# Router choice and sends of two batches moved from the tail into a scan, and a stage's first loads issued in the stage before it

## The chip, the cores and the metric

The kernel runs on one core of one Trainium2 chip. The metric is device time in microseconds (us) of one execution. Besides the time of plain runs there is one profiled execution, whose trace gives each instruction its start and duration. Engines are called as in the profile: PE (TensorE), DVE (VectorE), ACT (ScalarE), POOL (GpSimd) and SP (SyncE, which here only issues DMAs).

## What is computed

The reference works on x of 4 batches x 512 tokens x 512 features and a context of 4 x 512 x 256. Four layers are added to x in turn:

```python
x = x + _L0_xattn_ref(_layernorm(x), fside_BxS2xS2_0, ctx_1024)   # two int8-quantised linears, silu gate
x = x + _L0_ffn_ref(_layernorm(x), lut, gate_idx, up_idx, down_idx)  # weights = lut[idx], width 1376
x = x + _L1_xattn_ref(ctx_1024, _layernorm(x), ...)               # selective scan, 16 states x 512 channels
x = x + _L1_ffn_ref(_layernorm(x), gate_w, w_gate, w_up, w_down)  # 32 experts, 8 of them per token

def step(state, inp):                       # the scan, over the 512 positions
    d, b, c, u = inp
    dA = jnp.exp(d[..., None] * A)
    state = state * dA + (d * u)[..., None] * b[:, None, :]
    y = jnp.einsum('bdn,bn->bd', state, c)

probs = jax.nn.softmax(x @ gate_w, axis=-1)     # the expert layer, P = tokens * 8, E = 32
w, sel = jax.lax.top_k(probs, K)
pos = jnp.arange(P) - start[se]                 # a row's place among the rows of its expert
y = jnp.einsum('eci,eih->ech', silu(g) * u, w_down)
out = jnp.zeros((T + 1, H)).at[t_slot].add(w_slot[:, None] * y)
```

## The kernel before

The program is two blocks with a barrier of all engines between them. `front_block` computes the first layer, makes the looked-up weights of the second layer in 176 slots of a small PE product each, stores them to DRAM (`w_halves`), and stores what the scan reads: dt, du, u, the rows of B and C (`bc_rows`), and x after the first layer (`x_store`). SP issues nearly all DMAs of the block, in the order of its code. At its end SP waits for the landing of all stores of dt, u, B and C and x, and for the zero fills of the send buffer (`filled`, lines 369 to 373), so the barrier opens after the last store has landed.

`mix_and_experts_block` has three stages.

**The scan** runs 4 batches of 16 slots, slot g = 16 b + l (`UNITS` = 16). In a slot POOL makes the scan's input for the slot ahead (`inputs_product`, line 1441, B times du), ACT makes four decays exp(dt A) into a single PSUM bank (line 1895), DVE does four scans (line 2217) and two products with C (line 2225, after the second and the fourth scan), PE sums the states (line 1637). A decay waits for the scan before it, since both use the one bank. In the room beside that PE computes the second layer, from slot 3 of each batch on: `up` products (line 1611), `down` products (line 1625), with ACT and DVE forming the half between them. Layer norms, z gates and residuals are put in by slot number, as "asides" of ACT and lines between DVE's scans. SP issues the weight loads (`mix_wup`, `mix_wdn`) one or two halves ahead and the loads of B and C of the next batch in slots 13 to 15.

**The tail**, after the last slot: the last residual and z gate, and the router for all 16 tiles of 128 tokens. Per batch PE transposes the normalised rows and multiplies with `gw` (`choice_transposes`, `logits`), DVE subtracts the maximum (`shift`, line 2304), ACT takes the exponent, DVE finds the top 8 (`choose`), PE counts the ranks, DVE turns them into row numbers (`place`, line 2341 writes `where`). POOL then sends the rows: 128 indirect DMAs (`send`, line 1474), 16 tiles for each of k = 0 to 7, where k is the rank of the choice in the order of expert numbers. A token's k-th expert is never below k, so expert e can be loaded once the sends of k up to e are done; SP waits for that, for e under 8, and loads the tiles (line 1357).

**The experts**: 32 times, 576 rows each in five tiles: PE transposes (line 1763), gate and up (line 1793), down (line 1816), ACT writes the split activations (line 2015 once per half), the result goes back by DMA. The sends of k = 2 to 7 run beside the experts 0 to 5, each k after expert k-2's tiles are transposed. From expert 6 on POOL adds results to the output (line 1492).

## Time and profile before

| | us |
|---|---|
| median of 3 runs | 1883.29 (1882.07 to 1884.48) |
| the profiled execution | 1881.68 |
| its span in the trace | 1879.5 |
| first block, to the barrier | 0 to about 510 |
| scan | 533 to about 1181 |
| tail, to the first tile load | 1181 to 1239 |
| experts 0 to 6 | 1239 to about 1411 |
| the remaining experts, end | 1411 to 1879.5 |

Busy shares over the span: PE 83%, DVE 70%, ACT 48%, POOL 42%. The mean DMA rate is 237 GB/s.

In a timeline row stand the start (us from the span's start), the duration, the engine, the line, the operation with output<-input, and in brackets the idle time before it with what released it. A row of `SPq` is a DMA being issued, not its transfer. In a table of stretches stand the stretch, its length, the busy time and number of instructions of PE, PEld (weight loads), DVE, ACT and POOL, and then the granted PE clock (1.00 is 2.4 GHz), the DMA share of 16 engines and GB/s. A DMA row ends with KB each and the median us from issue to landing.

### The profile page before, as it was taken

The numbers are of one execution on the slowest core, as the hardware profiler recorded it, in microseconds if no ns is written. First come the engines' busy times: TensorE is split into PE (matmuls) and PEld (weight loads), VectorE is DVE, ScalarE is ACT, GpSimd is POOL, SyncE is SP. The second block draws the span as 40 slices with busy tenths as digits, with TensorE's granted clock in tenths as the row PEclk, the third lists the DMA queues.
The fourth block names the chain that finished last, engine by engine and source line by source line (L and its number), as shares of the span: only waits on it lengthen the run. The fifth ranks groups of instructions, "written<-read, shape, count | busy, mean of one in ns | idle before, by whom it ended". The sixth has DMA issues, their size and how long they took to land. (4 is left out here: it accounts for less than half of the span.)

```text
span 1879.5 us, 26432 instructions
## 1 busy us (share of the span) xinstructions
PE 1554.0 (83%) x9418; PEld 1319.2 (70%) x9426; DVE 1308.7 (70%) x1901; ACT 911.0 (48%) x1577; POOL 791.8 (42%) x481
## 2 busy tenths in 40 slices
PE   5857778677528987996898799975899999999896
PEld 3444355454428976895897689855789999999785
DVE  6677586786659989999998999642445555555452
ACT  3444545445234444344444534432466666666463
POOL 1010000010045456445655643177735766762555
PEclk9878888888758997997999799987999999999998
DMA  7988799984682492375359236379998999999876
GB/s 213 343 281 275 274 321 368 333 270 157 210 314 95 175 357 74 119 283 222 106 188 370 82 118 218 145 266 338 382 365 232 250 269 253 256 260 223 226 170 85
DMA packets 187942, 445.48 MB, mean 237 GB/s; under 512 B 41616, under 2 KB 43664, under 8 KB 177568
## 3 DMA queue, kind: packets, MB, share of 16 engines
q1 hardware_dynamic: 115040, 283.37, 44.7%
q0 software_dynamic: 31760, 74.48, 16.8%
q10 hardware_dynamic: 41008, 85.89, 12.6%
q8 instruction: 78, 1.28, 0.3%
q14 instruction: 56, 0.46, 0.1%
HBM read 246.77 MB, written 205.28 MB: 241 GB/s over the span
## 5 line engine op out<-in xcount | busy, mean ns | idle before, releaser
L1441 POOL TENSOR_TENSOR mix_st<-mix_Bb,mix_du 128x2048 f32<-128x2048 f32 x64 | 293.3, 4583 | 268.2 <-DVE mix_st L2225 255.7
L2217 DVE TENSOR_TENSOR_SCAN mix_st<-mix_YY,mix_st 128x512 f32<-128x512 f32 x256 | 312.0, 1219 | 46.0 <-POOL mix_st L1441 24.0
L1895 ACT ACTIVATE mix_YY<-mix_dt,mix_A 128x512 f32<-128x512 f32 x256 | 176.9, 691 | 276.5 <-DVE mix_st L2217 272.3
L1492 POOL DMA_INDIRECT out_x<-moe_ys,moe_meta x130 | 210.5, 1619 | 190.1 <-ACT moe_ys L2032 84.6
L1611 PE MATMUL mix_G<-mix_xThi,mix_wup 128*128 128x256 f32 x1408 | 273.0, 291 | 14.5 <-issue 13.6
L1611 PEld LDWEIGHTS mix_G<-mix_xThi,mix_wup 128*128 128x128 f32 x1408 | 231.8, 199 | 17.6 <-issue 16.2
L1793 PE MATMUL mix_Dp<-moe_xhi,moe_whi 128*128 128x288 f32 x768 | 234.5, 305 | 2.0 <-ACT moe_xhi L1995 1.5
L1793 PE MATMUL mix_Dp<-moe_xhi,moe_wlo 128*128 128x288 f32 x768 | 228.9, 298 | 0.0
L1793 PE MATMUL mix_Dp<-moe_xlo,moe_whi 128*128 128x288 f32 x768 | 228.7, 298 | 0.0
L2357 DVE TENSOR_TENSOR moe_xlo<-mix_G,moe_xhi 128x512 fp32r<-128x512 f32 (+1 forms) x160 | 102.2, 638 | 170.5 <-ACT moe_xhi L1995 167.9
L1637 PE MATMUL mix_YY<-mix_ident,mix_st 128*128 128x128 f32 x1024 | 145.1, 296 | 86.2 <-DVE mix_st L2225 86.2
L435 PE MATMUL front_L<-front_oh,front_pick 128*128 128x512 f32 x528 | 177.9, 475 | 45.0 <-ACT front_wst L582 28.6
L1611 PE MATMUL mix_G<-mix_xTlo,mix_wup 128*128 128x256 f32 x704 | 203.9, 290 | 0.0
L1637 PEld LDWEIGHTS mix_YY<-mix_ident,mix_st 128*128 128x128 f32 x1024 | 126.0, 153 | 99.3 <-issue 52.6
L742 DVE TENSOR_SCALAR front_oh<-front_idx,front_kcol 128x1536 fp32r<-128x1536 int32 x176 | 176.6, 1048 | 13.8 <-PE front_L L435 10.4
L435 PEld LDWEIGHTS front_L<-front_oh,front_pick 128*128 128x128 f32 x528 | 109.9, 220 | 94.7 <-DVE front_oh L742 39.6
L2225 DVE TENSOR_TENSOR mix_st<-mix_st,mix_Cb 128x1024 f32<-128x1024 f32 x128 | 161.5, 1262 | 1.1
L1793 PEld LDWEIGHTS mix_Dp<-moe_xhi,moe_whi 128*128 128x128 f32 x768 | 146.7, 191 | 8.1 <-issue 2.2
L1474 POOL DMA_INDIRECT x_by_expert<-moe_XB,moe_where x128 | 129.1, 1009 | 46.3 <-issue 38.9
L1793 PEld LDWEIGHTS mix_Dp<-moe_xlo,moe_whi 128*128 128x128 f32 x768 | 146.7, 191 | 2.3
L1793 PEld LDWEIGHTS mix_Dp<-moe_xhi,moe_wlo 128*128 128x128 f32 x768 | 146.4, 191 | 0.0
L2347 DVE TENSOR_TENSOR moe_wlo<-moe_raw,moe_whi 128x768 fp32r<-128x768 f32 (+1 forms) x96 | 100.2, 1045 | 64.0 <-ACT moe_whi L1984 64.0
(237 smaller groups left out, 3064.9 us busy)
## 6 DMA issues: line engine op xcount, KB each, us to landing
x_by_expert<-front_zeros ACTq DMA_DIRECT2D x16, 4480.0 KB, 24.1
mix_wup<-w_halves SPq DMA_DIRECT2D x44, 1024.0 KB, 5.5
moe_raw<-in_ew SPq DMA_DIRECT2D x32, 1280.0 KB, 8.5
moe_xt<-x_by_expert SPq DMA_DIRECT2D x128, 256.0 KB, 8.6
mix_wdn<-w_halves SPq DMA_DIRECT2D x44, 512.0 KB, 6.4
front_idx<-in_idx SPq DMA_DIRECT2D x44, 384.0 KB, 9.0
w_halves<-front_wst SPq DMA_DIRECT2D x44, 384.0 KB, 7.9
mix_Bb<-bc_rows SPq DMA_DIRECT2D x16, 1024.0 KB, 9.4
```

The source lines that it names most:

```text
L435: last = nc.tensor.matmul(L[:, n, :], pick[:, j, :, :].rearrange("p a n -> p (a n)"), oh[:, t % OH, n * S:(n + 1) * S], start=(j == 0), st ...
L742: nc.vector.tensor_scalar(oh[:, t % OH, :], idx[:, h % 2, :], kcol[:, j:j + 1], None, ALU.is_equal).then_inc(onehot_made, 1)
L1441: nc.gpsimd.tensor_tensor(st[:, g % STBUF, :, :], Bb[:, q, :, :], du[:, k % 2, :].unsqueeze(1).to_broadcast([P, NG, S]), ALU.mult).then_in ...
L1474: pool.indirect_dma_start(out=s["XG"], out_offset=bass.IndirectOffsetOnAxis(ap=where[:, i, k:k + 1], axis=0), in_=XB[:, i, :], in_offset=N ...
L1492: pool.indirect_dma_start(out=out_rows, out_offset=bass.IndirectOffsetOnAxis(ap=meta[0:rows, e % MBUF, j, 0:1].bitcast(U32), axis=0), in_= ...
L1611: last = nc.tensor.matmul(G[:, i % 2, v, :], wup[:, j % UPBUF, part, v * D + c * P:v * D + (c + 1) * P], x[:, c, cols], start=(n == 0), st ...
L1637: last = nc.tensor.matmul(Y[:, t, :], st[:, g % STBUF, n, t * P:(t + 1) * P], ident[:, :], is_transpose=True, start=(q == 0 and n == 0 and ...
L1793: last = nc.tensor.matmul(Dp[:, m % 4, 0:HALF_U], w[:, e % 2, at:at + P], x[:, e % 2, c, cols], start=(n == 0), stop=(n == len(steps) - 1))
L1895: nc.scalar.activation(dA, dt[:, k % 2, :], ACT.Exp, scale=A[:, c, m:m + 1]).then_inc(da_ready, 1)
L2217: nc.vector.tensor_tensor_scan(r, dA, r, 0.0, ALU.mult, ALU.add).then_inc(scanned, 1)
L2225: nc.vector.tensor_tensor(r, r, Cb[:, l % GROUPS, own, :], ALU.mult).then_inc(prod_ready, 1)
L2357: nc.vector.tensor_tensor(xlo[:, e % 2, :, at], T[:, n % 2, :].rearrange("p (c t) -> p c t", c=DC)[:, :, 0:rows], xhi[:, e % 2, :, at].bit ...
```

## The change

**Seam between the blocks.** `load_ahead` is new in the first block: at slot turn 170, behind the 19th pair of weight stores, SP waits for all stores of dt, u, B and C and issues the first loads of the scan (dt, du, four of B, x of batch 0; 5.5 MB) into SBUF which a new layout leaves free. The block's end waits for `filled` alone; the landing of x of the last batches (`x1_out`) is waited for in `load_x(b)` of the second block and by DVE before the first residual. In the second block SP's first issues are A, dskip and four loads of C; POOL's first instruction is the product of slot 0, ahead of the small memsets, which ACT and DVE wait for no longer.

**Early choice.** The router of batches 0 and 1 (`EARLY` = 2) is computed in batches 2 and 3 of the scan. PE: transposes of tile 0 and 1 in slot 15 of batches 1 and 2, of tile 2 and 3 and all logits in slot 0 of batches 2 and 3, ranks in slot 2. ACT: the copies of the transposes (`rows_to_columns`), the first of them ahead of the decay for the next slot; exponent in slot 1. DVE: shift, top 8 and mask in slot 1, place in slot 3, weights in slot 4. SP stores row numbers and weights behind the rows (`store_meta`, slot 5) and loads three of four tiles back (`load_waiting`).

**Sends in the scan.** 48 of the 128 sends (three tiles of each of the two batches, all k) are issued by POOL in slots 8 to 15 and the next slot 0 of batch 2, and in slots 9 to 15 and right behind the scan of batch 3. Each k after that has 10 sends instead of 16: two tiles of the early batches, four of batch 2, four of batch 3. The tail chooses for batches 2 and 3 alone.

```diff
+AHEAD_AT = 170
+SENDS_AT = ({8: 3, 9: 2, 10: 3, 11: 3, 12: 3, 13: 3, 14: 3, 15: 3, 16: 1}, {9: 2, 10: 3, 11: 3, 12: 3, 13: 3, 14: 3, 15: 3, 16: 4})
...
+            def load_ahead():
+                sp.wait_ge(bc_out, 16 * NB)
+                sp.wait_ge(u_out, 16 * NB)
+                sp.wait_ge(dt_out, 32 * NB)
+                sp.dma_start(dt[:, 0, :], s["DT"][0][:, 0, :]).then_inc(ahead_in, 16)
+                sp.dma_start(du[:, 0, :], s["DU"][0][:, 0, :]).then_inc(ahead_in, 16)
...
+                sp.dma_start(xt_mix[:, 0, :, :], s["X1"][0].rearrange("(t p) n -> p t n", p=P)).then_inc(ahead_in, 16)
...
-            sp.wait_ge(bc_out, 16 * NB)
-            sp.wait_ge(u_out, 16 * NB)
-            sp.wait_ge(dt_out, 32 * NB)
-            sp.wait_ge(x1_out, 16 * NB)
             sp.wait_ge(filled, 16 * (FILLS + 2))
...
+            def send_waiting(w, first, end):
+                if first == 0:
+                    pool.wait_ge(filled, 16 * (FILLS + 2))
+                    pool.wait_ge(waiting_in, 16 * w + 16)
+                    pool.wait_ge(where_ready, w + 1)
+                for j in range(first, end):
+                    k, n = divmod(j, STAGED)
+                    send(w * STAGED + n, k, waiting[w][:, n, :])
...
-            for k in range(TOP):
+            sends(EARLY, 0)
+            sends(EARLY + 1, 0)
+            for k in range(1, TOP):
                 if k > 1:
                     pool.wait_ge(e_xT_ready, NT * (k - 2) + 2)
-                for b in range(NB):
-                    sends(b, k)
+                sends_on_chip(k)
+                sends(EARLY, k)
+                sends(EARLY + 1, k)
...
+                    if l == UNITS - 1 and 0 < b <= EARLY and t == 3:
+                        rows_to_columns(b - 1, 0)
+                    if l == 0 and b >= EARLY and t != 1:
+                        rows_to_columns(b - 2, max(1, t))
+                    if l == 1 and b >= EARLY and t == 1:
+                        exponent(b - 2)
...
+                if l == 1 and b >= EARLY:
+                    choose_top(b - 2)
+                if l == 3 and b >= EARLY:
+                    place_key(b - 2)
+                if l == 4 and b >= EARLY:
+                    row_weights(b - 2)
```

On SP around the barrier, from the last store of the first block on, before (`x_store` is x after the first layer; lines 155, 64, 63 and 1212 are the wait and the barrier):

```order
L329 DMA x_store<-front_xt 128x4x512 [waits front_x1_ready]
L155 UNCONDITIONAL_BRANCH [waits front_x1_out,front_dt_out,rows_filled,front_u_out,front_bc_out]
L64 UNCONDITIONAL_BRANCH [waits barrier_Pool_Activation_PE_DVE_SP_release]
L67 ISA
L63 UNCONDITIONAL_BRANCH
L1212 UNCONDITIONAL_BRANCH [waits barrier_Pool_Activation_PE_DVE_SP_release]
L1274 DMA mix_A<-in_alog 128x64
L1275 DMA mix_dskip<-in_dskip 128x4
L1219 DMA mix_dt<-dt_store 128x512
L1222 DMA mix_du<-du_store 128x512
L1233 DMA mix_Bb<-bc_rows 128x2048
```

And now:

```order
L366 DMA mix_dt<-dt_store 128x512 [waits front_dt_out,front_u_out,front_bc_out]
L367 DMA mix_du<-du_store 128x512
L369 DMA mix_Bb<-bc_rows 128x2048 x4
L371 DMA mix_xt<-x_store 128x4x512
L317 DMA w_halves<-front_wst 64x1536 [waits front_evicted]
...
L343 DMA x_store<-front_xt_111 128x4x512 [waits front_x1_ready]
L162 UNCONDITIONAL_BRANCH [waits rows_filled]
L64 UNCONDITIONAL_BRANCH [waits barrier_Pool_Activation_PE_DVE_SP_release]
...
L1373 DMA mix_A<-in_alog 128x64
L1374 DMA mix_dskip<-in_dskip 128x4
```

The loads of dt, du, B and x stand ahead of the last weight stores and of the barrier, and the wait for `x1_out` is gone.

On PE at the end of slot 15 of batch 1 and in slot 0 of batch 2, before (`mix_G` by `wup` is an up product, `mix_Dp` by `wdn` a down product, `mix_YY` by `mix_st` the sum of states):

```order
L1611 MATMUL mix_G<-mix_xThi,mix_wup 128x256
L1637 MATMUL mix_YY<-mix_ident,mix_st 128x128 x16
L1644 MATMUL mix_YY<-mix_ident,mix_u 128x128 x4
L1625 MATMUL mix_Dp<-mix_wdn,mix_hhi 128x512 x2
L1625 MATMUL mix_Dp<-mix_wdn,mix_hlo 128x512
```

And now (line 1808 is an early transpose, line 1822 the logits):

```order
L1747 MATMUL mix_G<-mix_xThi,mix_wup 128x256
L1808 MATMUL mix_G<-mix_ident,mix_x_3853 128x128 x4
L1773 MATMUL mix_YY<-mix_ident,mix_st 128x128 x8
L1808 MATMUL mix_G<-mix_ident,mix_x_3853 128x128 x4
L1773 MATMUL mix_YY<-mix_ident,mix_st 128x128 x8
L1780 MATMUL mix_YY<-mix_ident,mix_u 128x128 x4
L1808 MATMUL mix_G<-mix_ident,mix_x_3853 128x128 x4
L1822 MATMUL mix_G<-mix_gw,mix_y 128x32 x8
L1761 MATMUL mix_Dp<-mix_wdn,mix_hhi 128x512 x2
```

The first transposes stand behind the last up product of slot 15, and the logits ahead of the down products of slot 0.

On POOL in slots 8 and 9 of batch 2, before:

```order
L1441 TENSOR_TENSOR mix_st<-mix_Bb,mix_du 128x2048 [waits late_unit_done,late_prod_ready,late_b_in1,late_dt_du_in0]
L1441 TENSOR_TENSOR mix_st<-mix_Bb,mix_du 128x2048 [waits late_unit_done,late_prod_ready,late_b_in2,late_dt_du_in0]
L1447 TENSOR_TENSOR mix_rstd<-mix_mv,mix_eps_col 128x4 [waits late_var_ready2]
L1448 TENSOR_TENSOR mix_rstd<-mix_rstd,mix_power 128x4 [waits late_pool_link]
L1449 TENSOR_TENSOR mix_nmr<-mix_mv,mix_rstd 128x4 [waits late_pool_link]
L1450 TENSOR_TENSOR mix_nmr<-mix_zero,mix_nmr 128x4 [waits late_pool_link]
L1441 TENSOR_TENSOR mix_st<-mix_Bb,mix_du 128x2048 [waits late_unit_done,late_prod_ready,late_b_in3,late_dt_du_in0]
```

And now:

```order
L1535 TENSOR_TENSOR mix_st<-mix_Bb,mix_du 128x2048 [waits late_unit_done,late_prod_ready,late_b_in1,late_dt_du_in0]
L1581 DMA x_by_expert<-mix_waiting_3859,mix_where 33024x560 [waits late_where_ready,late_waiting_in,rows_filled]
L1581 DMA x_by_expert<-mix_waiting_3859,mix_where 33024x560 x2
L1535 TENSOR_TENSOR mix_st<-mix_Bb,mix_du 128x2048 [waits late_unit_done,late_prod_ready,late_b_in2,late_dt_du_in0]
L1549 TENSOR_TENSOR mix_rstd<-mix_mv,mix_eps_col 128x4 [waits late_var_ready2]
...
L1581 DMA x_by_expert<-mix_waiting_3859,mix_where 33024x560 x2
L1535 TENSOR_TENSOR mix_st<-mix_Bb,mix_du 128x2048 [waits late_unit_done,late_prod_ready,late_b_in3,late_dt_du_in0]
```

The sends stand between two products of POOL, two or three to a slot.

## Rows read from the trace of the kernel before

**Rows 1.** Busy time, clock, DMA share and rate of three stretches

```profile
510.00:1181.00 671.00, 558.01 (x3866) 519.95 (x3867) 604.19 (x779) 296.64 (x534) 346.11 (x127) 0.89 0.54 196
...
1393.00:1848.00 455.00, 449.63 (x2967) 405.52 (x2966) 244.73 (x405) 281.11 (x532) 258.23 (x150) 0.99 0.95 237
...
1306.00:1328.00 22.00, 17.70 (x104) 15.56 (x105) 8.01 (x14) 9.38 (x18) 16.81 (x18) 0.92 1.03 380
```

**Rows 2.** Timeline of DVE: the first scan

```profile
533.21 1.22 DVE L2217 TENSOR_TENSOR_SCAN mix_st<-mix_YY,mix_st 128x512 f32<-128x512 f32 x1 [23.99 <-POOL mix_st L1441]
```

**Rows 3.** Timeline of SP, ACT and POOL around the barrier

```profile
496.88 12.83 SPq L303 DMA_DIRECT2D w_halves<-front_wst  x4
509.75 1.21 SPq L329 DMA_DIRECT2D x_store<-front_xt  x1
519.57 0.33 SPq L1274 DMA_DIRECT2D mix_A<-in_alog  x1
...
526.07 0.69 ACT L1895 ACTIVATE mix_YY<-mix_dt,mix_A 128x512 f32<-128x512 f32 x1 [3.81 <-DMA mix_du<-du_store]
...
528.62 4.49 POOL L1441 TENSOR_TENSOR mix_st<-mix_Bb,mix_du 128x2048 f32<-128x2048 f32 x1 [8.30 <-DMA mix_Bb<-bc_rows]
```

**Rows 4.** DMA issues from 505 to 521 us: KB each, median us to landing

```profile
x_store<-front_xt SPq DMA_DIRECT2D x1, 1024.0 KB, 7.4
...
mix_A<-in_alog SPq DMA_DIRECT2D x1, 32.0 KB, 1.8
```

**Rows 5.** Timeline of ACT and PE where batch 1 ends

```profile
849.14 0.69 ACT L1895 ACTIVATE mix_YY<-mix_dt,mix_A 128x512 f32<-128x512 f32 x1 [1.28 <-DVE mix_st L2217]
...
851.53 1.91 PE L1637 MATMUL mix_YY<-mix_ident,mix_st 128*128 128x128 f32 x16
...
859.44 1.06 PE L1637 MATMUL mix_YY<-mix_ident,mix_st 128*128 128x128 f32 x8 [2.79 <-DVE mix_st L2225]
```

**Rows 6.** Two stretches of the tail: DVE's top 8 with weights, and place

```profile
1200.49:1202.54 2.05, 2.05 (x21) 2.05 (x21) 1.91 (x17) 0.60 (x1) 1.08 (x3) 1.00 0.00 0
1206.86:1208.11 1.25, 1.25 (x14) 1.25 (x14) 1.15 (x8) 0.47 (x1) 0.92 (x3) 1.00 1.03 383
```

**Rows 7.** DVE products: all in the scan, one beside POOL, experts with and without sends

```profile
L2225 DVE TENSOR_TENSOR mix_st<-mix_st,mix_Cb 128x1024 f32<-128x1024 f32 x128 | 161.5, 1262 | 1.1
...
897.87 2.07 DVE L2225 TENSOR_TENSOR mix_st<-mix_st,mix_Cb 128x1024 f32<-128x1024 f32 x1
...
L2347 DVE TENSOR_TENSOR moe_wlo<-moe_raw,moe_whi 128x768 fp32r<-128x768 f32 x10 | 9.6, 964 | 7.2 <-ACT moe_whi L1984 7.2
...
L2347 DVE TENSOR_TENSOR moe_wlo<-moe_raw,moe_whi 128x768 fp32r<-128x768 f32 x45 | 43.0, 956 | 40.6 <-ACT moe_whi L1984 40.6
```

**Rows 8.** Timeline of POOL: a product of the scan

```profile
830.48 4.62 POOL L1441 TENSOR_TENSOR mix_st<-mix_Bb,mix_du 128x2048 f32<-128x2048 f32 x1 [5.43 <-DVE mix_st L2225]
```

**Rows 9.** Landing of the up weights: whole span, then 1005 to 1020 us

```profile
mix_wup<-w_halves SPq DMA_DIRECT2D x44, 1024.0 KB, 5.5
...
mix_wup<-w_halves SPq DMA_DIRECT2D x2, 1024.0 KB, 8.8
```

**Rows 10.** The sends: their group on the page, and the fifth of them

```profile
L1474 POOL DMA_INDIRECT x_by_expert<-moe_XB,moe_where x128 | 129.1, 1009 | 46.3 <-issue 38.9
...
1221.26 0.97 POOL L1474 DMA_INDIRECT x_by_expert<-moe_XB,moe_where  x1 [6.83 <-DVE moe_where L2341]
```

**Rows 11.** Timeline of SP: the tile loads of expert 0

```profile
1238.67 2.39 SPq L1357 DMA_DIRECT2D moe_xt<-x_by_expert  x5
```

**Rows 12.** Timeline of ACT: first split activation of experts 0, 7 and 8

```profile
1255.78 0.45 ACT L2015 ACTIVATE moe_chl<-moe_hc 64x288 fp32r<-64x288 f32 x1 [0.26 <-DVE moe_hc L2368]
...
1421.33 0.43 ACT L2015 ACTIVATE moe_chl<-moe_hc 64x288 fp32r<-64x288 f32 x1
...
1438.92 0.43 ACT L2015 ACTIVATE moe_chl<-moe_hc 64x288 fp32r<-64x288 f32 x1
```

**Rows 13.** Queue of the sends from 1306 to 1328 us: packets, MB, share

```profile
q0 software_dynamic: 1286, 4.61, 52.4%
```

More of the change, by code:

```diff
@@ L959, in downs_of_slot, with mix_and_experts_block @@
     return early + halves_of_slot(g - 2)
-def mix_and_experts_block(nc, d, s, out, filled, w_out):
+def mix_and_experts_block(nc, d, s, out, filled, w_out, x1_out, ahead_in, ahead):
     ALL = NB * UNITS
@@ L1926, in normalise @@
                     act.wait_ge(zT_ready, TT * (b - 1))
+                    if b == NB - 1 and t == 0:
+                        for k in range(TOP):
+                            act.wait_ge(sent[k], 16 * STAGED)
                 nc.scalar.activation(xn[:, t, :], x[:, t, :], ACT.Identity, bias=nmr[:, w, t:t + 1],
@@ L1969, in exponent @@
                 act.wait_ge(shifted, b + 1)
-                own = pr[:, b * TT:(b + 1) * TT, :]
-                nc.scalar.activation(own, own, ACT.Exp).then_inc(exp_ready, 1)
+                nc.scalar.activation(pr(b), pr(b), ACT.Exp).then_inc(exp_ready, 1)
             def weights_high(e, c):
@@ L2310, in choose, with choose_top, choose_mask @@
+                nc.vector.tensor_tensor(pr(b), lg, over_experts(mx(b)), ALU.subtract).then_inc(shifted, 1)
+            def choose_top(b):
                 dve.wait_ge(exp_ready, b + 1)
-                for i in tiles:
-                    last = nc.vector.max(top[:, i, :], pr[:, i, :])
+                for t in range(TT):
+                    last = nc.vector.max(top(b)[:, t, :], pr(b)[:, t, :])
                 link(last)
-                for i in tiles:
-                    last = nc.vector.match_replace(rest[:, i, :], top[:, i, :], pr[:, i, :], -1.0)
+            def choose_mask(b):
+                for t in range(TT):
+                    last = nc.vector.match_replace(rest(b)[:, t, :], top(b)[:, t, :], pr(b)[:, t, :], -1.0)
@@ L2316, in choose @@
                 link(last)
[L2317 removed]
+                nc.vector.tensor_scalar(masks(b), rest(b), 0.0, None, ALU.is_lt).then_inc(mask_ready, 1)
             def row_weights(b):
[L2320 to L2322 removed]
@@ L2323, in row_weights @@
-                nc.vector.tensor_tensor(XB[:, own, D + 1:D + 1 + E_N], pr[:, own, :], over_experts(total[:, own]),
-                                        ALU.mult).then_inc(meta_ready, 1)
-            def place(b):
-                own = slice(b * TT, (b + 1) * TT)
-                tiles = range(b * TT, (b + 1) * TT)
+                link(nc.vector.tensor_reduce(total(b), top(b), AX_X, ALU.add))
+                link(nc.vector.reciprocal(total(b), total(b)))
+                to = meta_of(b)[:, :, 1:META] if b < EARLY else XB[:, b * TT:(b + 1) * TT, D + 1:D + META]
@@ L2335, in place, with place_rows, choose @@
                 dve.wait_ge(mask_ready, b + 1)
-                link(nc.vector.scalar_tensor_tensor(out=key[:, own, :], in0=key[:, own, :], scalar=-1.0,
-                                                    in1=mask[:, own, :], op0=ALU.mult, op1=ALU.mult))
-                for i in tiles:
-                    last = nc.vector.max(near[:, i, :], key[:, i, :])
-                link(last)
-                nc.vector.tensor_scalar(where[:, own, :], near[:, own, :], -1.0, AWAY, ALU.mult, ALU.add).then_inc(where_ready, 1)
+                link(nc.vector.scalar_tensor_tensor(out=key(b), in0=key(b), scalar=-1.0, in1=masks(b),
+                                                    op0=ALU.mult, op1=ALU.mult))
+            def place_rows(b):
+                for t in range(TT):
+                    last = nc.vector.max(near(b)[:, t, :], key(b)[:, t, :])
+                link(last)
+                nc.vector.tensor_scalar(where[:, b * TT:(b + 1) * TT, :], near(b), -1.0, AWAY, ALU.mult,
+                                        ALU.add).then_inc(where_ready, 1)
+            def choose(b):
+                choose_top(b)
+                choose_mask(b)
+            def place(b):
+                place_key(b)
+                place_rows(b)
             def weights_low(e, c):
```

514 lines of the change are left out of this document (322 added, 192 removed).

## The prediction

> **What bounds the kernel now.** I first read the table of stretches, because each stage has a limit of its own. In the scan DVE is busy 604 of 671 us and DMA has half its time free; in the late experts PE is busy 450 of 455 us, so nothing but PE's work counts there; in a stretch of the early experts PE has only 17.7 of 22 us and DMA is full at 380 GB/s [rows 1]. Then the timelines at the two seams. Between the blocks DVE stands idle for 24.0 us before its first scan at 533.21 [rows 2]. From the tail to the early experts I follow one mark, ACT's first split activation of an expert: expert 0 has it at 1255.78, expert 7 at 1421.33 and expert 8 at 1438.92 [rows 12]. An expert that waits for nothing takes 17.6 us; the seven before took 165.6 instead of 7 x 17.6 = 123.1, so 42.4 us are lost there, beside the tail itself. So three places matter: seam 1, the tail with experts 0 to 6, and the scan, which now gets more work.
>
> **Seam 1.** Before, the last store of x is issued at 509.75 and the first DMA of the second block at 519.57 [rows 3]; the store takes 7.4 us from its issue to landing [rows 4], so it is in at 517.15 and from there to the first issue are 2.4 us of barrier. The change takes that landing out of the barrier. SP gets there when the issue of the store ends, at 509.75 + 1.21 = 510.96 [rows 3]; with the same 2.4 the second block opens at 513.3. B and du are then in SBUF: their loads are 5.5 MB, at 380 GB/s [rows 1] 15 us, and stand ahead of the last four weight stores, which before were issued from 496.88 on [rows 3]. So POOL's product of 4.49 us [rows 3] ends at 517.8. ACT's first decay needs A: its load took 1.8 us on a free queue [rows 4], but now it stands behind the megabyte of x. I take it as landed at 517.3 to 517.9; two small instructions and the decay of 0.69 [rows 3] put the first scan at 519.4. The Trainium skill, DMA: Bandwidth & Descriptors, Queues (HWDGE ordering), says that on each DMA engine descriptors are consumed in ring order; by that rule A is behind x, with no rule A would be in at 515.1 and the product would decide, at 517.8. The sum goes by 519.4, with ends 517.8 and 519.9: 533.21 - 519.4 = 13.8. A wait of 0.7 on the load of u and the short waits for the other B loads go too: **-14.5**, from -16 to -8 if the barrier still ends with the landing. The loads' price in the first block is their issue on SP, 7 issues at under 1.2 us [rows 3] ahead of weight stores for which nobody is waiting: nothing, as PE and DVE there don't wait for SP. What is late next is the wait of DVE for `x1_out` before the first residual, hundreds of us later: nothing.
>
> **Tail.** Before, the fifth send, the first of batch 1, starts at 1221.26, 6.8 us idle and right behind the second batch's row numbers, and the tile loads of expert 0 are issued at 1238.67 [rows 10, 11]. Between are 11 more sends at 1.009 + 0.3 us = 1.28, and one landing. In the changed order batch 3 stands where batch 1 stood, with one shift and one set of weights fewer ahead, about 2.5 us: its rows are ready at about 1217.7 and its weights at 1218.4. By then batch 2's sends and the on-chip tiles' are out. Four sends (5.1 us) end at 1223.7; the load follows the last send's end by 1.9 us as before: 1225.6, **13.1** earlier.
>
> **Experts 0 to 6.** In 22 us of the early experts DMA moved 8.35 MB by 22 x 380 GB/s [rows 1], 4.61 MB of it the 16 sends of one k [rows 13]. With 10 sends, 2.88 MB, an expert has some 6.5 MB, at the same rate 17.1 us. By POOL it is 10 x 1.28 = 12.8 us instead of 20.5 [rows 10]. Both are under PE's 17.6, the first only just. I let expert 0 have its mark 13.1 earlier, at 1242.7; expert 1 takes 20.3, since PE is still at its lower clock and the loads bunch up; six at 17.6 would put expert 7 at 1368.6, 52.7 before 1421.33 [rows 12]. For a limit so near I add 5 us of waits: 1374, so tail and experts together give **-47**. Ends: -55 with no waits and a better expert 1, -30 if an expert still takes 21 us. From expert 7 on the pace is PE's in both.
>
> **What the scan pays.** (1) The first early transposes stand behind the last up product of slot 15. ACT's copy of them stands ahead of the decay for the next slot, which ran at 849.14; the up products end and PE's next group starts at 851.53 [rows 5]. So ACT waits until about 852.1, copies 0.6, and the decay starts at 852.7 to 852.9 and the scan behind it at 853.5 instead of 850.75: 2.65 us, twice: **+5.3** (bounds +2, if DVE's asides fill the hole, and +6). (2) DVE's own new work where it is the bound: the same work in the tail took 2.05 (top 8, mask, weights) and 1.25 (place) [rows 6]. With 0.1 of a wait that is 3.4 for a batch; the shift hides in DVE's wait for ACT. Twice, and 0.4 once for the last row: **+7.2** (0 to +9; slots in which PE is the bound would hide it, but slots 1 to 4 aren't such). (3) PE's transposes, logits and ranks are 4.6 us per batch, most in slot 0, where PE had idle times of 2.8 and 1.4 [rows 5] and none is waited for: 0, without this cover +2 a batch. (4) The sends: POOL has 5.4 us idle beside a 4.6 us product in a slot [rows 8] and three sends are 3.8: hidden, and POOL's product is a slot ahead. (5) Their bytes, 0.86 MB in a slot that had up to 400 GB/s in slots 13 to 15: up weights landed in 5.5 us and in 8.8 where B and C were loaded [rows 9]. I put +1 for late weights in batch 2 and +0.5 for ACT's wait for the 24 sends at the start of the last z path. Sum of the scan: 5.3 + 7.2 + 1.5 = **+14**, from +8 to +25.
>
> **The sum.** -14.5 - 47 + 14 = -47.5. The profiled execution took 1881.7, of which the span is 1879.5; 1881.7 - 47.5 = 1834.2. The median of the runs is 1.6 above the profiled one, so **1836 us**. The case's own range is 1826 to 1846.
>
> **Rival A: the early experts stay bound by DMA.** For it: DMA is at full share in them, and 17.1 is half a microsecond from PE's pace, with results and the next raw weights coming in bursts. Against it: a quarter of the bytes is gone. If an expert takes 21 us, seven take 147 instead of 165.6: 18.6, and 13.1 of the tail, 31.7 in all: 1836 + 15 = 1851.
>
> **Rival B: sends and DVE's products hold each other up.** The one product of the scan that began beside a POOL product took 2.07 us, against 1.26 in the mean [rows 7]. If the sends did the same to both products of a slot, 16 slots x 2 x 0.81 = 26 us at most; the sends fill under half of the time in which the products can fall: about 12 to 26, so 1848 to 1862, I say 1858. Against it: DVE's two-input operation on 768 columns took 964 ns in the stretch with sends and 956 without [rows 7]. The Trainium skill, SBUF — State Buffer, SBUF: two separate sides, says that a DVE operation with two SBUF inputs locks the shared port pair only against a GpSimd operation that reads SBUF, and its box on DVE and DMA lets only DVE's operations in a two-port mode starve the descriptors. By that a send costs a product nothing, by its general lock it would; the trace agrees with the first (964 and 956), so B has a small chance.
>
> **Rival C: the scan turns to its weight loads, slower than before.** The place is PE's up product, which waits for `mix_wup`. Loads are one to two slots of about 10 us ahead, and land in 5.5 to 8.8 [rows 9]. With 0.86 MB of sends more per slot they could land later than 13 us; then every us more stalls PE and with it DVE. The gain of 61.5 at the seams less the 12.5 of the early choice is 49; the 16 slots with sends must lose over 3 us each to turn it round, so landings of over 16 us: 1890. Against it: 0.86 MB at 380 GB/s is 2.3 us, and in slots 8 to 12 DMA is half idle.
>
> **Rival D: better than forecast.** The chain in slot 15 costs less, expert 1 follows at 18, no DMA limit: 1822.
>
> **That the change doesn't do what it says** can be at seam 1 alone: another engine or `filled` may end the barrier late. It costs 6 of the 14.5: 1842, within the first case.
>
> **How the numbers follow.** Forecast 0.60, A 0.20, B 0.08, C 0.04, D 0.08. The predicted time is that of the first. The range must reach to A and D, with the ends of the unknown costs around A: 1820 to 1857; left out are C, and part of B and of the ends. A measurement of this kernel can tell about 0.2%, 3.8 us. Every case but C is faster by more than that: faster 0.94; between C and the others lies a strip with 0.02; slower 0.04.
>
> **What would show it.** Right: the first scan near 519.4 and its idle time ended by ACT, not POOL; the slot behind slot 15 of batches 1 and 2 longer by 2 to 3 us with ACT waiting for PE; no product of POOL starting later than it would by DVE; the tile loads of expert 0 about 13 us nearer to the end of the scan; marks of experts 1 to 7 under 18.5 us apart and PE's waits for tiles in the early experts below 15 us. Wrong: marks over 20 us apart with DMA full (A); DVE's products over 1.5 us in slots 8 to 15 of batches 2 and 3 (B); PE idle there with the up weights as releaser (C); first scan after 524, or the scan over 20 us longer, by a chain that I have not seen between ACT's copies and PE in slot 0.

## The result

| | before | changed |
|---|---|---|
| median of 4 runs each | 1882.88 us | 1837.78 us (1835.89 to 1838.54) |
| the profiled execution | 1881.68 | 1838.54 |
| its span in the trace | 1879.5 | 1836.8 |

The ratio is 0.9758, with a 95% interval from 0.9741 to 0.9775: 45 us faster. The prediction was 1836, with a range from 1820 to 1857. The total was right to 2 us; the terms of its sum were not all, as the marks show. A mark is the same event in both traces:

| mark | before | changed | gain so far |
|---|---|---|---|
| last store of x issued (first block) | 509.75 | 511.46 | -1.7 |
| first scan | 533.21 | 520.64 | 12.6 |
| POOL's product 16 (first slot of batch 1) | 676.84 | 662.04 | 14.8 |
| last product of the scan on DVE | 1177.40 | 1175.69 | 1.7 |
| tile loads of expert 0 | 1238.67 | 1227.50 | 11.2 |
| first split activation, expert 0 | 1255.78 | 1245.93 | 9.9 |
| the same, expert 1 | 1294.27 | 1272.26 | 22.0 |
| the same, expert 7 | 1421.33 | 1379.75 | 41.6 |
| end | 1879.5 | 1836.8 | 42.7 |

So seam 1 gives 16.5 us when counted from the store of x (the first block itself ended 1.7 later), the scan takes 13.1 of it away, the tail gives 9.5, the experts 0 to 7 give 30.4, and the rest 1.1.

### The profile page after: what moved, and what is told of

Read it like the earlier page. It is cut to its first block and busy times, and to the rows that moved or that the text cites. A ratio compares the mean times of both kernels' runs of the same rounds, so it can differ in the third digit from the quotient of the medians.

```text
span 1836.8 us, 26417 instructions
## 1 busy us (share of the span) xinstructions
PE 1548.2 (84%) x9418; PEld 1317.3 (72%) x9426; DVE 1312.9 (71%) x1901; ACT 910.5 (50%) x1577; POOL 798.9 (43%) x485
## 3 DMA queue, kind: packets, MB, share of 16 engines
q8 instruction: 78, 1.28, 0.3%
## 5 line engine op out<-in xcount | busy, mean ns | idle before, releaser
L765 DVE TENSOR_SCALAR front_oh<-front_idx,front_kcol 128x1536 fp32r<-128x1536 int32 x176 | 176.6, 1048 | 13.9 <-PE front_L L458 10.3
L2398 DVE TENSOR_TENSOR mix_st<-mix_st,mix_Cb 128x1024 f32<-128x1024 f32 x128 | 165.7, 1295 | 0.9
L1747 PEld LDWEIGHTS mix_G<-mix_xTlo,mix_wup 128*128 128x128 f32 x704 | 140.1, 199 | 1.4
## 6 DMA issues: line engine op xcount, KB each, us to landing
mix_wdn<-w_halves SPq DMA_DIRECT2D x44, 512.0 KB, 7.1
```

Source lines behind the costliest of these rows:

```text
L765: nc.vector.tensor_scalar(oh[:, t % OH, :], idx[:, h % 2, :], kcol[:, j:j + 1], None, ALU.is_equal).then_inc(onehot_made, 1)
L1747: last = nc.tensor.matmul(G[:, i % 2, v, :], wup[:, j % UPBUF, part, v * D + c * P:v * D + (c + 1) * P], x[:, c, cols], start=(n == 0), st ...
L2398: nc.vector.tensor_tensor(r, r, Cb[:, l % GROUPS, own, :], ALU.mult).then_inc(prod_ready, 1)
```

## The profile of the changed kernel

**Seam 1.** Timelines of SP, ACT and POOL, to be read against [rows 2, 3]:

```profile
511.46 1.22 SPq L343 DMA_DIRECT2D x_store<-front_xt  x1
515.00 0.35 SPq L1373 DMA_DIRECT2D mix_A<-in_alog  x1
...
515.02 4.50 POOL L1535 TENSOR_TENSOR mix_st<-mix_Bb,mix_du 128x2048 f32<-128x2048 f32 x1 [18.98 <-POOLq L63]
...
519.27 0.26 ACT L2040 ACTIVATE mix_A<-mix_A 128x64 f32<-128x64 f32 x1 [2.98 <-DMA mix_dskip<-in_dskip]
...
520.64 1.22 DVE L2390 TENSOR_TENSOR_SCAN mix_st<-mix_YY,mix_st 128x512 f32<-128x512 f32 x1 [9.73 <-ACT mix_YY L2055]
```

From the store's issue to the first DMA of the second block are now 3.5 us, before 9.8. POOL starts at once and is ready at 519.5; ACT waits for the two small loads, A and dskip, until 519.27, and the first scan is released by ACT and no longer by POOL. These loads, issued at 515.00 and 515.40, show how long they took behind the megabyte of x. The page of DMA issues from 508 to 522 us (KB each, median us to landing) has

```profile
x_store<-front_xt SPq DMA_DIRECT2D x1, 1024.0 KB, 7.4
...
mix_A<-in_alog SPq DMA_DIRECT2D x1, 32.0 KB, 3.4
mix_dskip<-in_dskip SPq DMA_DIRECT2D x1, 2.0 KB, 3.8
```

3.4 us where the same load took 1.8 on a free queue [rows 4]. The store landed at 511.46 + 7.4 = 518.9, A 0.4 us ahead of it at 518.4 and dskip 0.4 behind it at 519.2, all within one us, though their sizes are 1024, 32 and 2 KB.

**Where slot 15 ends.** Batch 1 to 2, DVE and ACT (line 2137 is the copy of the transposes), against [rows 5]:

```profile
837.88 0.60 ACT L2137 ACTIVATE mix_y<-mix_G 128x512 f32<-128x512 f32 x1 [4.31 <-PE mix_G L1808]
838.37 0.69 ACT L2055 ACTIVATE mix_YY<-mix_dt,mix_A 128x512 f32<-128x512 f32 x1
...
839.16 1.22 DVE L2390 TENSOR_TENSOR_SCAN mix_st<-mix_YY,mix_st 128x512 f32<-128x512 f32 x1 [2.62 <-ACT mix_YY L2055]
```

ACT stands 4.3 us for PE's transposes, and DVE 2.62 us for ACT. In batch 3 the wait is 2.97.

**Sends in the scan.** POOL and DVE in slots 10 and 11 of batch 2:

```profile
946.66 1.85 POOL L1581 DMA_INDIRECT x_by_expert<-mix_waiting,mix_where  x1 [0.49 <-issue]
948.82 0.99 POOL L1581 DMA_INDIRECT x_by_expert<-mix_waiting,mix_where  x1 [0.30 <-issue]
949.83 4.62 POOL L1535 TENSOR_TENSOR mix_st<-mix_Bb,mix_du 128x2048 f32<-128x2048 f32 x1
954.62 1.79 POOL L1581 DMA_INDIRECT x_by_expert<-mix_waiting,mix_where  x1 [0.17 <-issue]
...
946.37 1.21 DVE L2398 TENSOR_TENSOR mix_st<-mix_st,mix_Cb 128x1024 f32<-128x1024 f32 x1
...
952.60 2.95 DVE L2398 TENSOR_TENSOR mix_st<-mix_st,mix_Cb 128x1024 f32<-128x1024 f32 x1
```

The first send starts at 946.66, within DVE's product, and takes 1.85 us, to 0.9 behind the product's end at 947.58; alone a send takes 0.97. With that POOL's own product starts at 949.83, without any wait before it, and is still running when DVE's next product starts at 952.60: that one takes 2.95 us, to 1.1 behind the end of POOL's at 954.45. From there POOL does a product and three sends every 9.5 us without a gap; four more of DVE's products in this batch take 1.37 to 1.58, two in the next 2.92 and 1.56.

**Tail.** The four sends of batch 3 for k = 0 and the load behind them, against [rows 10, 11]:

```profile
1217.98 2.94 DVE L2530 TENSOR_TENSOR moe_wlo<-moe_raw,moe_whi 128x768 fp32r<-128x768 f32 x3
1218.66 3.11 POOL L1581 DMA_INDIRECT x_by_expert<-moe_XB,mix_where  x1 [6.30 <-DVE moe_XB L2498]
1222.08 0.98 POOL L1581 DMA_INDIRECT x_by_expert<-moe_XB,mix_where  x1 [0.30 <-issue]
...
1227.50 2.48 SPq L1457 DMA_DIRECT2D moe_xt<-x_by_expert  x5
```

The first of them takes 3.11 us instead of 0.97, again to 0.85 behind the end of DVE's three subtractions (1220.92).

What sets the time at which batch 3 is ready is PE. The changed kernel has 20 filler products there (`stay_busy(20, ...)`, line 1852, whose result nobody reads), and the transposes of the last batch stand behind them:

```profile
1200.57 6.16 PE L1852 MATMUL mix_G<-mix_onesb 128*128 128x512 bf16 x20
1206.57 1.04 PE L1797 MATMUL mix_G<-mix_ident,moe_XB 128*128 128x128 f32 x8
```

ACT had the first two tiles ready at 1201.8, and stood 5.4 us for these transposes.

**Early experts.** Two stretches, the early experts and the late ones, with the columns of [rows 1], and ACT's marks of experts 1, 2 and 3:

```profile
1304.00:1326.00 22.00, 22.00 (x146) 19.68 (x144) 12.13 (x21) 14.52 (x28) 13.24 (x13) 1.00 1.01 363
1364.00:1810.00 446.00, 441.15 (x2913) 398.29 (x2912) 238.69 (x396) 275.37 (x521) 257.56 (x152) 0.99 0.94 230
```

In a stretch as long as that from 1306 to 1328 of before PE is now busy all the time (22.0 of 22 instead of 17.7), at 363 GB/s and with DMA still full. The marks are at 1272.26, 1290.60, 1308.19, 1325.78, 1344.68, 1362.26 and 1379.75: 18.3, 17.6, 17.6, 18.9, 17.6, 17.5 apart, PE's own pace. What is left of waits for tiles is small:

```profile
PE mix_G L1924 <- DMA moe_xt<-x_by_expert: 11.1, 5, 4.8
```

This row of waits from 1225 to 1400 us (total, times, longest) was 36.5 us in 15 times before.

## Experiments

The first eight ran in two groups beside runs of the kernel before at 1882.7 and 1881.9 us. Of each I give the marks too, each counted from an earlier mark of the same trace. Up to the end of the scan such a distance moves by hundredths where nothing changes; that from the scan to the loads of expert 0 moves by about one us, with the granted clock of PE's fillers, and that from expert 0 to expert 1 by 2 us.

**Seam 1 undone whole and in half.** `seam_off` puts the loads behind the barrier (`load_column(0, 0)`, `load_b(0, q)` and `load_x(0)` in the second block, in the order of before) and has the first block wait for x again; `x1_wait` does only the second:

```diff
+            sp.wait_ge(x1_out, 16 * NB)
             sp.wait_ge(filled, 16 * (FILLS + 2))
```

> The changed kernel with seam 1 alone as before: the loads of dt, du, B and x of batch 0 are issued behind the barrier, in the order of before, and the first block waits for the landing of x. My theory (two seams and a scan that add up): first scan 14 to 15 us later, at about 535, every later mark later by the same, the time 14.5 us above the changed kernel (1852). Rival (the gain of seam 1 is given back in the scan, since later slots are bound by PE): the first scan is 14 later, but the end of the scan and the time move by under 5.

> The changed kernel in which the first block waits again for the landing of x; the loads stay ahead. My theory: the barrier opens at the landing plus 2.4 us, so POOL's first product moves from 515.0 to about 521 and the first scan from 520.6 to about 526.0, 5 to 6 us; the time 5.5 above (1843). Rival (another engine or the zero fills end the barrier, and the landing never did): 0 to 1 us.

Measured: `seam_off` 1852.59 us (0.9844, from 0.9827 to 0.9860), 14.8 above the changed kernel. `x1_wait` 1840.65 (0.9783, from 0.9767 to 0.9799), 2.9 above where 5.5 was expected; by time alone it can't be told from the changed kernel. SP in `x1_wait` and in `seam_off`:

```profile
508.52 1.22 SPq L343 DMA_DIRECT2D x_store<-front_xt  x1
518.15 0.35 SPq L1374 DMA_DIRECT2D mix_A<-in_alog  x1
```

```profile
509.16 1.22 SPq L343 DMA_DIRECT2D x_store<-front_xt  x1
518.76 0.33 SPq L1369 DMA_DIRECT2D mix_A<-in_alog  x1
```

The first block does not end at the same time in two profiles. Counted from the issue of its last store: the second block opens after 9.8 us before, 9.6 in both of these, 3.5 in the changed kernel; the first scan comes after 23.5 before, 23.2 in `seam_off`, 14.2 in `x1_wait`, 9.2 in the changed kernel; POOL's product 16 starts after 167.1 before, 166.9 in `seam_off`, 155.6 in `x1_wait`, 150.6 in the changed kernel. So the landing of x is worth 5.0 and the loads ahead 11.3 us. The expected 5.5 for the former holds for this distance alone: the first scan came at 522.70 and not at 526.0, only 2.1 later than in the changed kernel, since the first block ended 2.9 earlier in this profile. The rival of `seam_off`, that the scan gives the gain back, falls: its last product of the scan comes at 1189.54 against 1175.69.

**The sends of the scan, moved back or left out.** `sends_back` keeps the early choice and sends all 128 tiles' rows behind the scan, 16 for each k; `sends_out` leaves the 48 sends away:

```diff
-SENDS_AT = ({8: 3, 9: 2, ...}, {9: 2, 10: 3, ...})
+SENDS_AT = ({}, {})
...
-                for i in range(2 * STAGED, EARLY * TT):
+                for i in range(EARLY * TT):
                     send(i, k, XB[:, i, :])
```

(The second hunk in `sends_back` alone. Both also leave out ACT's wait for the early sends, and in `sends_out` the experts wait for the 10 sends that are left.)

> The changed kernel with the early choice kept in the scan, but all 48 early sends back behind the scan: 16 sends for each k, all tiles loaded to XB. My theory (fewer sends per k give the experts' pace, the early choice gives the tail): the tile loads of expert 0 stay at about 1227, since the eight early tiles are sent while the tail computes; from expert 0 to expert 7 the marks are 160 to 166 us apart again instead of 133.8; the time 28 to 34 above the changed kernel (1866 to 1872). Rival (bytes are not the cause, the early experts wait for other loads or for the clock): experts 0 to 7 stay under 145 apart, time within 8.

> The changed kernel without the 48 sends in the scan: they are left out altogether, so the rows of six tiles do not reach the experts; 10 sends for each k as in the changed kernel. My theory (the sends are hidden in the scan, although POOL's products come later and DVE's products beside them are longer): the end of the scan moves by under 1.5 us and the time by under 3; DVE's long products (2.95 and 1.56 us) are gone. Rival B (sends and products hold each other up and the scan pays): end of the scan 5 to 12 us earlier.

Measured: `sends_back` 1875.67 us (0.9957, from 0.9943 to 0.9971), 37.9 above the changed kernel. Experts 0 to 7 are 166.6 us apart (133.8 changed, 165.5 before), and from 1306 to 1328 us the row is that of before again, PE 16.1 of 22 and DMA full:

```profile
1306.00:1328.00 22.00, 16.08 (x92) 13.91 (x91) 7.23 (x12) 7.63 (x14) 16.82 (x18) 0.84 1.01 375
```

So the sends beside the early experts make their pace. Whether by their bytes or by POOL's time to issue them is not shown, since 16 sends instead of 10 raise both, and the trace of the kernel before speaks for POOL in part. There POOL issues sends without a pause, and the last send of a k ends every 20.4 to 21.4 us, from 1236.8 for k = 0 to 1383.8 for k = 7: 147 us of the 165.6. The loads of an expert are issued only behind them. The longest wait of PE, 13.3 us, ends 3.2 us after the loads of expert 2 were issued (its sends ended at 1278.4), and in the 20 us before that DMA was not full (0.85):

```profile
1260.00:1280.00 20.00, 7.83 (x41) 5.78 (x39) 5.69 (x9) 5.95 (x11) 15.12 (x17) 0.69 0.85 307
1280.27 0.82 SPq L1357 DMA_DIRECT2D moe_xt<-x_by_expert  x2
1283.48 1.11 PE L1763 MATMUL mix_G<-mix_ident,moe_xt 128*128 128x128 f32 x4 [13.28 <-DMA moe_xt<-x_by_expert]
```

From expert 2 on DMA is full and the third tile of an expert lands 9 to 12 us after its issue, so there the bytes count too. In the changed kernel the 10 sends of a k take 12.5 to 13.2 us and POOL waits for PE between them (19.6 us from 1225 to 1400).

But in `sends_back` the loads of expert 0 came at 1237.74, 10 late, against the expectation: eight sends stood on POOL ahead of the last scale (line 1557), 1201.10 to 1211.43, and the whole chain of the last tiles behind it. That is a fault of the experiment's order, and this term is not to be read from it.

`sends_out` 1830.60 us, with the last product of the scan at 1175.59 against 1175.69 (0.4 us nearer to the first scan), and no product of DVE above 1.3 us in the slots that had sends (930 to 1010 and 1105 to 1175 us). So the long products there are the sends' doing, and yet the scan pays next to nothing for them. The time moved by 7.2 us and not by under 3 as expected, but that says nothing of the scan: the mark of expert 7 is at 1381.05, later than in the changed kernel, and the end of the profile all the same 4 us earlier. What shortens the work behind it was not looked for; rows are missing there, too.

**ACT's copy behind the decay.** `copy_late`:

```diff
-                    if l == UNITS - 1 and 0 < b <= EARLY and t == 3:
-                        rows_to_columns(b - 1, 0)
...
                 decay(NG * g + 4)
+                if l == UNITS - 1 and 0 < b <= EARLY:
+                    rows_to_columns(b - 1, 0)
```

> The changed kernel with ACT's first copy of the early transposes behind the decay for the next slot instead of ahead of it, in slot 15 of batches 1 and 2. My theory (this copy's place is the whole of DVE's new wait of 2.6 us there): the wait of the first scan of batch 2 falls from 2.62 to under 0.3; part comes back as a wait of the second scan, 0.6 to 1; each batch gains 1.6 to 2.6, the last product of the scan comes 3 to 5 us earlier, relative to the first scan. Rival (PE is late there in any case and only the name of the wait changes): under 1 us.

Measured: 1831.61 us (0.9735, from 0.9718 to 0.9752), 6 below the changed kernel, though the two intervals still touch. The wait is gone:

```profile
833.50 1.21 DVE L2390 TENSOR_TENSOR_SCAN mix_st<-mix_YY,mix_st 128x512 f32<-128x512 f32 x1
```

From POOL's product 33 to 34 are 11.97 us instead of 13.46 (before 11.18), from 49 to 50 12.10 instead of 13.81; from the first scan to the last product the scan takes 651.9 us instead of 655.1. 3.2 of the 5.6 come back; for the rest ACT now stands 2.34 us for the transposes ahead of the second decay, and DVE 1.11 us for ACT. Of the 6 us of time only these 3.2 belong to the edit's place: expert 1 came 23.6 us behind expert 0 instead of 26.3, for which I have no cause.

**A send beside DVE.** `low_late` holds DVE's subtractions back until the sends of k = 0 have landed; `plain_dma` puts a plain DMA of POOL's queue ahead of the first send of batch 3:

```diff
+            dve.wait_ge(sent[0], 16 * TILES)
             for c in range(3):
                 weights_low(0, c)
```

```diff
+            pool.wait_ge(norm_ready[2], TT * NB)
+            pool.wait_ge(meta_ready, NB)
+            pool.dma_start(s["XN"][NB - 1][0:P, :], XB[:, 12, :]).then_inc(merged, 16)
             sends(EARLY + 1, 0)
```

> The changed kernel with DVE's three subtractions for expert 0's weights held back until the 16 sends of k = 0 have landed. Theory P (a send that starts beside a DVE operation with two SBUF inputs waits for its end): the first send of batch 3 takes 1.0 us instead of 3.11, the tile loads of expert 0 come 2.1 us earlier relative to the end of the scan. Rival (a send after an idle stretch, or with new tiles, is slow by itself): it stays at 3.1 and nothing moves.

> The changed kernel with one plain DMA more on POOL's queue (128 rows of one tile to a part of DRAM that nobody reads), put right ahead of the first send of batch 3, where DVE runs three subtractions with two SBUF inputs. If writing descriptors is what waits for the port, the plain DMA takes 2.5 us or more, to the end of the subtractions plus 0.9, and the send behind it 1.0. If only a send's reading of its row numbers waits, the plain DMA takes about 1 us and the send behind it ends 0.9 behind the subtractions.

Measured: `low_late` 1835.45 us (0.9752, from 0.9734 to 0.9771), 2.3 below the changed kernel, which the intervals don't separate. In the trace the send is short:

```profile
1217.90 0.97 POOL L1581 DMA_INDIRECT x_by_expert<-moe_XB,mix_where  x1 [7.24 <-DVE moe_XB L2498]
1219.17 0.98 POOL L1581 DMA_INDIRECT x_by_expert<-moe_XB,mix_where  x1 [0.30 <-issue]
```

From the start of that send to the loads of expert 0 are 7.1 us instead of 8.8. But counted from the last product of the scan these loads come only 0.8 us earlier (51.0 instead of 51.8), not the expected 2.1. The rest went ahead of the send: PE's 20 fillers took 7.03 us at a mean granted clock of 0.63 here, 6.16 at 0.72 in the changed kernel, and the last batch's weights were ready 43.0 us behind the last product instead of 42.1. `gate_again` below has the same edit with fillers of 6.16 us and weights at 42.1; there the loads come 1.9 us earlier. `plain_dma`, of which there is one execution:

```profile
1217.28 2.94 DVE L2533 TENSOR_TENSOR moe_wlo<-moe_raw,moe_whi 128x768 fp32r<-128x768 f32 x3
1217.68 0.61 POOL L1666 DMA_DIRECT2D xn_store<-moe_XB  x1 [6.84 <-DVE moe_XB L2501]
1218.59 2.54 POOL L1581 DMA_INDIRECT x_by_expert<-moe_XB,mix_where  x1 [0.30 <-issue]
1221.43 0.97 POOL L1581 DMA_INDIRECT x_by_expert<-moe_XB,mix_where  x1 [0.30 <-issue]
```

The plain DMA starts within the subtractions and is issued in 0.61 us; the send behind it ends at 1221.13, 0.9 behind the subtractions' end (1220.22). So it isn't the writing of descriptors as such that waits for DVE, but something that an indirect send does and a plain one doesn't. Reading its row numbers from SBUF is the one such thing that the program shows; that it is this was not tried apart.

**Both edits, and the gate of the sends.** `best` is `copy_late` with `low_late`. `gate_later` and `gate_again` are `best` with

```diff
-                    pool.wait_ge(e_xT_ready, NT * (k - 2) + 2)
+                    pool.wait_ge(e_xT_ready, NT * (k - 2) + (2 if k == 2 else NT))
```

> copy_late and low_late together. Theories as in these: 3 to 5 us from the scan and 2 from the tail, 5 to 7 us below the changed kernel (1831 to 1833). Rivals: no gain of either, 1838.

> gate_later once more, since in its first run DMA delivered less in the stage of the sends for every kernel, the one before too (290 instead of 357 GB/s over 100 us). Theory A (the sends beside them slow the tile loads of experts 1 and 2): against best the mark of expert 2 comes 2 to 4 us earlier relative to the tile loads of expert 0, time 1828. Rival (the sends, held back, end later, and the loads that wait for them too): a mark of experts 3 to 7 comes later than in best, time 1832 to 1838.

Measured: `best` 1831.43 us (0.9732, from 0.9716 to 0.9747), its loads of expert 0 50.5 us behind the last product of the scan (51.8 changed, 61.3 before). It is the fastest with `copy_late`, from which it cannot be told: what the send gains, expert 1 gives back (26.8 us behind expert 0; 23.6 in `copy_late`, 26.3 changed). `gate_again` 1836.81 (0.9756), on another chip beside a kernel before of 1882.14: expert 2 comes 63.0 behind the loads of expert 0 instead of 62.4, and experts 0 to 7 are 138.7 apart instead of 134.4. Its theory falls, the rival holds, as far as one profile on another chip tells.

**A group in which all was slower.** `after_again` (the changed kernel as it is), `sends_back2` and `gate_later` ran in a group in which the kernel before took 1940.37 us, too. They are compared among themselves alone. The scan took 656.3 us instead of 655.1 in `after_again`; the loss lies in the stage of the sends. There DMA moved 286 GB/s from 1240 to 1340 us instead of 357, and the expectation of `gate_again` above reads this as slower DMA, for the kernel before too. The traces don't bear that out: DMA was less busy there (0.81 instead of 0.98), and PE waited for tiles 4.2 us instead of 11.1, but PE, DVE and ACT stood idle with no releaser in the trace (PE 10.1 and DVE 44.1 us from 1225 to 1400, in the changed kernel none). The landings of that stage are missing in this trace, so what held the engines stays open. The kernel before was not traced in this group.

> The changed kernel once more, as it is, beside the two others: 1836 to 1839. It says how much a second profile differs and gives the others a partner of the same chip. Both theories of the slip of 1.7 us at the end of the first block: chance (the store of x is issued somewhere from 507.5 to 512 in all profiles, this one too), or the loads ahead (it is issued at 511 or later again).

> As sends_back, but six of the eight early sends of k = 0 stand behind the last scale, so that they do not delay it. My theory (the tail's gain comes from the early choice, the pace of the experts from fewer sends): tile loads of expert 0 at 1227 to 1230, no longer at 1237.7; experts 0 to 7 still 163 to 168 apart; time 29 to 34 above the changed kernel, about 1868. Rival (the tail's gain too comes from the early sends): loads of expert 0 at 1235 or later, time as sends_back, 1875.

> best, with the sends of k = 3 to 7 held back until all five tiles of expert k - 2 are transposed instead of two. Theory A (in the first experts the tile loads are slow because the next sends run beside them): marks of expert 1 and 2 come 2 to 4 us earlier, time 1828. Rival (the sends, held back, end later and the loads that wait for them too): marks of experts 3 to 7 move up to 20 us apart, time 1835 or more.

Measured: `after_again` 1870.84 us (0.9637) and not 1836 to 1839, experts 0 to 7 159.9 apart; in this group the change is worth 69.5 us and not 45. Its store of x was issued at 507.27, in the profiles of the changed kernel and its variants from 507.3 to 512.0: the slip of 1.7 us in the first block is chance. `sends_back2`, with six of the eight early sends behind the last scale, 1925.86, 55 above `after_again` where 29 to 34 were expected, with experts 0 to 7 193.2 apart where 163 to 168 were; the idle time without releaser is larger still here. Its loads of expert 0 come 57.6 us behind the last product of the scan (51.4 in `after_again`), but DVE stood idle for 9.2 and 3.4 us there with no releaser in the trace, where the changed kernel shows 6.3 and 0.5 behind PE. Whether the tail needs the early sends as well as the early choice stays open. `gate_later` 1856.52 (0.9569), 14.3 below `after_again`; `best` did not run in this group, so what the gate did here can't be told.

## Why the prediction was right, and where not

**Seam 1: the mechanism right, the second term small.** 13.8 for the first scan was 14.3, counted from the store of x. The other term, 0.7 for waits in the first slots, was 2.2. The barrier's own 2.4 us were right (3.5 from issue to open, of which 1.2 is the issue). By the rule on ring order that I weighed (the Trainium skill, DMA: Bandwidth & Descriptors, Queues, rings and completion order) A is behind x. It landed with x, 0.4 us ahead of it, and dskip 0.4 behind; that is nearer to the rule than to a free queue, but no run separates order from a queue that is merely full. POOL did not decide, and the scan started at 520.64 less the slip of 1.7, 518.9 against 519.4.

**The scan: 14 predicted, 13.1 measured.** The wait at slot 15 was 2.62 and 2.97 against 2.65. In POOL's product starts batch 2 shows 2.3 for slot 15, then 1.3, 1.0 and 1.3 in the slots of choice, place and weights, 5.9 in all against 6.05; batch 3 6.5. The 1.5 for the sends was wrong, it is at most 0.4: `sends_out`. The reason is not the one I gave. I had them hidden because POOL has room, 4.6 and three times 1.28 in a slot of 9.1. But a send beside DVE is longer (1.8, 1.1 and 1.2 us in a typical slot), so POOL has none left with 9.5 us of work; its product comes 2 us late and DVE's product runs into it. Slot 10 of batch 2 takes 10.9 us for that, the next four 9.5 each, where they took 9.1, 9.1, 9.9, 10.0 and 10.3 before. In the slots of 10 us DVE had room before (in one of them 9.15 of 10.3 us busy, and PE all of it), and there the lateness ends.

**Tail: 13.1 predicted, 9.5 measured.** The step that failed is the end of its chain: "Four sends (5.1 us) end at 1223.7". One of the four took 3.11 us, since DVE's next subtractions for the experts now start together with it: 2.1 us, of which `best` against `copy_late` and `gate_again` against the changed kernel take 2 and 1.9 away. The other 1.5 are the batch's row numbers and weights, 42.1 us behind the last product of the scan where I had 41.0, and half a microsecond to the first send. I had counted that chain by DVE's work; it goes by PE's 20 fillers, and follows them from profile to profile. Where the fillers start alike, 24.9 us behind the last product, the weights are ready at 41.7 us with fillers of 5.74 us (`seam_off`), at 42.1 with 6.16 and at 43.0 with 7.03. A kernel with fewer fillers there was not run.

**Experts: 33.9 predicted, 30.4 measured.** The 5 us put in for waits from expert 1 on were 2.0 (107.5 us for six experts, 105.5 at PE's pace); expert 1 came 26.3 behind expert 0 and not 20.3, and expert 0 1.3 later behind its loads. So the term that was too small is expert 1: PE stood idle for 7.3 us between these two marks, 4.8 of them for one tile load, and its granted clock was 0.88. The pace behind it held, 17.6 by PE, and rival A with its 21 us did not come. The reason that I gave, 17.1 by the bytes against 17.6, is only argued: the change took POOL's issue of a k from 20.5 to 12.8 us as well, and no run changes one without the other.

**Rival B** was half true. Sends and products do hold each other up, but by way of POOL's late product and with next to no cost to the scan. My argument against it looked at the wrong side: DVE's subtractions took 964 ns with sends and 956 without because it is the send that waits. The trace of the kernel before had it already:

```profile
1322.94 0.96 DVE L2347 TENSOR_TENSOR moe_wlo<-moe_raw,moe_whi 128x768 fp32r<-128x768 f32 x1 [1.74 <-ACT moe_whi L1984]
1323.06 1.69 POOL L1474 DMA_INDIRECT x_by_expert<-moe_XB,moe_where  x1 [0.30 <-issue]
```

All nine sends that start within such a subtraction there end 0.85 us behind the end of it, hidden in a mean of 1009 ns. Nor was 897.87 "the one product of the scan that began beside a POOL product": eight took over 1.3 us, two of them beside POOL's product of the scan (2.37 and 1.38 us), six beside a smaller multiplication of POOL (2.06 to 2.08). The Trainium skill, SBUF — State Buffer, SBUF: two separate sides, says that two SBUF inputs of DVE lock the port pair against a GpSimd operation that reads SBUF. I took a send for one that doesn't. If reading the row numbers counts, which no run shows, the rule fits all that was measured: the send waits (3.11, 2.54, 1.79 us), the plain DMA doesn't (0.61), and POOL's product and DVE's exclude each other (2.95 and 1.58).

**The sum.** In the profile the change gave 42.7 us, not 47.5: tail and experts were 7.1 too large; seam 1 was 2.0 too small, the scan 0.9, 1.1 behind expert 7 was in no term, and 1.7 went to the chance of the first block. The medians lie 45.1 apart, so part of the closeness of 1836 to 1837.8 is luck.

## What to carry to other kernels

Where the sends of a stage make its pace and an earlier stage has POOL and DMA half idle, moving sends is worth the difference of the two paces, here 30 us for 48 sends (13.8 MB), as long as what is left per step, in bytes and in POOL's time to issue, stays under the step of the next bound. A full DMA does not say which of the two it was: look when the loads are issued, and behind what. In the stage that takes the work, the cost came from one ordering, an eviction put ahead of the operation that the critical engine waits for, and next to nothing from the sends: look first at what each engine has to do in order just ahead of the recurrence. And cost an indirect DMA on GpSimd with the DVE instructions that will run at the moment it starts, not with its mean.

## What the runs showed of the hardware

- An indirect DMA of POOL that starts while DVE runs an operation with two SBUF inputs ends 0.85 to 0.93 us behind that operation's end (up to 1.85 us instead of 0.97 behind one operation; 3.11 and 2.54 where three stood in a row and it waited for the last; but one at 1228.93 in the kernel before waited only for the first of two, 1.45). One that starts within a subtraction with one input in PSUM (`moe_xlo`) took 0.97 or 0.98, in all 29 cases of the two kernels. One that starts 0.3 us ahead of DVE's product took 1.00, and the product 1.20. A plain DMA of POOL's queue was not held up (0.61).
- A DVE product with two SBUF inputs that starts beside POOL's product of 4.6 us ends 1.1 us behind it (2.95, 2.92, 1.58, 1.56).
- A 32 KB and a 2 KB load issued 3.5 and 3.9 us behind a store of 1 MB on the same queue took 3.4 and 3.8 us, alone 1.8 and 1.7.
- The first block, nearly the same program each time, ended at up to 4.7 us difference in fourteen profiles; marks should be counted from a common event.
- In one group of runs the kernel before took 58 us more and the changed kernel 33. The trace of the changed kernel there shows idle time without releaser on PE, DVE and ACT in the stage of the sends, and DMA less busy than else (0.81 instead of 0.98); the cause stays open.
